# First attention of a macaron network on one core: the scores of the first 128 keys move into one product for four heads, and VectorE takes over the sum of maxima and queries

## The reference, cut to what matters

```
Q, K, V = heads(xn @ Wq), heads(xn @ Wk), heads(xn @ Wv)      # xn = layernorm(x)
scores  = einsum('bhqd,bhkd->bhqk', Q, K) * 8 ** -0.5
scores  = where(key > query, -1e6, scores)
attn    = einsum('bhqk,bhkd->bhqd', softmax(scores), V)
x       = x + attn @ Wo + bo
```

## Time and profile before

| | |
|---|---|
| median of 3 runs | 2064.63 us (2064.27 to 2064.72) |
| the profiled execution, and its span | 2066.3 us, 2064.3 us |
| busy share of the span | PE 96%, DVE 79%, ACT 58%, POOL 45% |
| attn0 | 331 to 711 us; a chunk inside the stage takes 45.8 us |

### The profile page before, as it was taken

The page is one execution under the profiler, slowest core; times in us unless marked ns, Lnnn a source line. Parts: engine busy times, 40 slices in busy tenths (PEclk is TensorE's granted clock), DMA queues, the critical chain, the costliest instruction groups (busy, mean ns, idle before and its releaser), DMA issues.

```text
span 2064.3 us, 44740 instructions
## 1 busy us (share of the span) xinstructions
PE 1985.8 (96%) x10752; PEld 1438.8 (70%) x10752; DVE 1632.7 (79%) x3337; ACT 1200.7 (58%) x1736; POOL 930.1 (45%) x904
## 2 busy tenths in 40 slices
PE   6999998999999999999999999998999999999998
PEld 4777776666666677777877888874333357787787
DVE  7777777777777577777588888886777788888887
ACT  6667664555555577676554445445767764454544
POOL 4665663333332366666544444442122334444444
PEclk9999999999999999999999999999999999999999
DMA  6333343333232243444311111114233301111112
GB/s 210 101 122 113 108 120 112 98 97 96 82 91 82 55 130 118 130 129 114 112 37 47 41 46 46 45 43 138 84 130 104 120 28 46 47 46 41 41 51 72
DMA packets 120701, 179.29 MB, mean 87 GB/s; under 512 B 33840, under 2 KB 38576, under 8 KB 120496
## 3 DMA queue, kind: packets, MB, share of 16 engines
q1 hardware_dynamic: 120624, 178.37, 29.3%
HBM read 147.10 MB, written 31.20 MB: 86 GB/s over the span
## 4 chain that ended last, share of the span: by engine, by line
PE 64%; DVE 11%; issue 11%; POOL 9%; ACT 3%; DVEq 1%; POOLq 1%; DMA 0%; SPq 0%; ACTq 0%
PE pair L397 14%; PE pair L399 13%; PE pair L398 13%; POOL h_lo L1364 6%; PE bank L651 5%; PE pair L740 3%; PE bank L629 3%; PE pair L762 3%; PE pair L823 2%; PE bank L397 2%; PE bank L399 1%; PE bank L398 1%; DVE rmax L1188 1%; DVE h_hi L1131 1%; POOL rstd L1284 1%
## 5 line engine op out<-in xcount | busy, mean ns | idle before, releaser
L1370 POOL TENSOR_TENSOR h_lo<-hid,h_hi 128x512 fp32r<-128x512 f32 x256 | 335.5, 1311 | 410.4 <-ACT h_hi L920 410.1
L397 PE MATMUL pair<-xnT_hi,w_hi 128*128 (+1 forms) x1040 | 420.0, 404 | 2.6 <-DVE prod L1110 1.3
L1364 POOL TENSOR_TENSOR h_lo<-hid,h_hi 128x512 fp32r<-128x512 f32 x256 | 332.3, 1300 | 194.6 <-ACT h_hi L886 193.4
L399 PE MATMUL pair<-xnT_hi,w_lo 128*128 (+1 forms) x1040 | 407.7, 392 | 0.0
L398 PE MATMUL pair<-xnT_lo,w_hi 128*128 (+1 forms) x1040 | 407.4, 392 | 0.0
L915 ACT ACTIVATE hid<-pair,bias 128x512 f32<-128x512 f32 x256 | 176.6, 690 | 315.5 <-PE pair L399 273.8
L397 PE MATMUL pair<-h_hi,w_hi 128*128 128x512 f32 x784 | 311.5, 397 | 14.5 <-DVE h_lo L1133 6.2
L399 PE MATMUL pair<-h_hi,w_lo 128*128 128x512 f32 x784 | 306.5, 391 | 0.0
L398 PE MATMUL pair<-h_lo,w_hi 128*128 128x512 f32 x784 | 305.9, 390 | 0.0
L1131 DVE TENSOR_SCALAR h_hi<-pair,nb 128x512 fp32r<-128x512 f32 x256 | 191.2, 747 | 69.8 <-PE pair L399 67.1
L938 ACT ACTIVATE probs<-pair 128x1024 f32<-128x1024 f32 x160 | 163.5, 1025 | 130.2 <-PE pair L762 127.0
(11 more groups left out here) (164 smaller groups left out, 3234.4 us busy)
## 6 DMA issues: line engine op xcount, KB each, us to landing
wb<-parts_dram SPq DMA_DIRECT2D x512, 128.0 KB, 2.9
wb<-parts_dram SPq DMA_DIRECT2D x128, 256.0 KB, 3.3
parts_dram<-attn_parts SPq DMA_DIRECT2D x96, 256.0 KB, 2.9
attn_q_st<-parts_dram SPq DMA_DIRECT2D x64, 256.0 KB, 2.7
k_one<-parts_dram SPq DMA_DIRECT2D x128, 64.0 KB, 2.5
attn_k_st<-parts_dram SPq DMA_DIRECT2D x32, 256.0 KB, 3.0
stage_w<-in_w_dram SPq DMA_DIRECT2D x32, 130.0 KB, 2.4
stage_w<-in_w_dram SPq DMA_DIRECT2D x5, 512.0 KB, 6.6
```

The source lines that it names most:

```text
L397: eng.matmul(o, w_hi_, v_hi, start=start, stop=False, **kw)
L399: return eng.matmul(o, w_lo_, v_hi, start=False, stop=stop, **kw)
L1364: eng.tensor_tensor(h_lo[:, p % NH0, :], hid[:, unit_of(p) % NHID, :] if p else hs[:, :], h_hi[:, p % NH0, :].bitcast(F32), ALU.subtract). ...
L1370: eng.tensor_tensor(h_lo[:, j % NH1, :], hid[:, j // 2 % NHID, :], h_hi[:, j % NH1, :].bitcast(F32), ALU.subtract).then_inc(lo1p_ready, 1)
```

## The change

- Fills 2 and 3 by query keep block 2 against 384 keys and lose block 0. Each fill of two heads is now two products, and fill 4 two products of 512 columns, each over two heads, in place of four of 256.
- Block 0 of all four heads is one product of 512 columns and one mask product of 512 (`first_block_by_query`). It goes into bank 1 of the pair whose bank 0 takes the maxima's rows, which was unused. DVE reduces it (`first_block_maximum`).
- `maxima_to_rows` loses its product with the identity; DVE adds the rows in PSUM to `q_st` in place (`rows_to_stack`), and ACT's copy goes.
- The maxima's step moves to the end of slots 3, 8, 13 and 18. It carries the rows of the quad as before, and the first block of the quad after it. Its pair is free again when DVE has reduced the first block.

```diff
-Q_FILLS = ((0, ((3, 0),)), (1, ((3, 0),)), (0, ((2, 0), (0, 384))), (1, ((2, 0), (0, 384))), (None, ((1, 0),)))
+Q_FILLS = ((0, 3), (1, 3), (0, 2), (1, 2), (None, 1))
-MAX_AT = (4, 9, 14, 19)
-USES = tuple(u for n in range(NS0) for u in (("q", n),) + ((("max", n),) if n in MAX_AT else ()) + (("k", n),))
+MAX_AT = (3, 8, 13, 18)
+USES = tuple(u for n in range(NS0) for u in (("q", n), ("k", n)) + ((("max", n),) if n in MAX_AT else ()))
...
+            for half in range(2):
+                if fill == NF - 1:
+                    both = pair[b][:, half, :].rearrange("p (h s) -> p h s", h=2)
+                    eng.matmul(both, q, mem0.k_one[:, quad, half:QUAD:2, 0:w], start=True, stop=True, skip_group_check=True)
+                else:
+                    eng.matmul(pair[b][:, half, 0:w], q, mem0.k_one[:, quad, 2 * Q_FILLS[fill][0] + half, 0:w],
+                               start=True, stop=True, skip_group_check=True)
...
+        def first_block_by_query(eng, ch, quad, b):
+
+            o = pair[b][:, 1, :].rearrange("p (h s) -> p h s", s=P)
+            eng.matmul(o, mem0.q_st[:, quad, 0:P], mem0.k_one[:, quad, :, 0:P], start=True, stop=True, skip_group_check=True)
+            eng.matmul(o, identb, neg.unsqueeze(1).broadcast_to([P, QUAD, P]), start=False, stop=True, skip_group_check=True).then_inc(s0_ready, 1)
+
         def maxima_to_rows(eng, ch, quad, b):
 
             eng.wait_ge(neg_max.sem, 2 * (NQ * ch.g + quad + 1))
-            eng.matmul(pair[b][:, 0, :], ident_r[:, :], mem0.q_st[:, quad, :], start=True, stop=False, skip_group_check=True)
...
+            if n in MAX_AT and in_chunk(ch, ("max", n)):
+                eng.wait_ge(*last_reader(ch, ("max", n)))
+                maxima_to_rows(eng, ch if max_quad(n) < NQ else ch.after(), max_quad(n) % NQ, ring(("max", n)))
+                if first_block_of(ch, n) is not None:
+                    first_block_by_query(eng, *first_block_of(ch, n), ring(("max", n)))
...
-            eng.activation(mem0.q_st[:, quad, :], pair[b][:, 0, :], ACT.Copy).then_inc(q_full, 1)
...
-                eng.tensor_reduce(q[:, 2, heads], src[:, :, 0:384], AX_X, ALU.max)
-                eng.tensor_reduce(q[:, 0, heads], src[:, :, 384:S], AX_X, ALU.max).then_inc(s_used, 1)
+                qt = Q_FILLS[fill][1]
+                eng.tensor_reduce(q[:, qt, heads], src[:, :, 0:(qt + 1) * P], AX_X, ALU.max).then_inc(s_used, 1)
...
+        def first_block_maximum(eng, ch, quad, b):
+
+            eng.wait_ge(s0_ready, NQ * ch.g + quad + 1)
+            eng.tensor_reduce(mem0.rmax[:, quad % 2, 0, :], pair[b][:, 1, :].rearrange("p (h s) -> p h s", s=P),
+                              AX_X, ALU.max).then_inc(s0_used, 1)
+
+        def rows_to_stack(eng, ch, quad, b):
+
+            eng.wait_ge(q_ps, NQ * ch.g + quad + 1)
+            eng.tensor_tensor(mem0.q_st[:, quad, :], pair[b][:, 0, :], mem0.q_st[:, quad, :].bitcast(F32), ALU.add).then_inc(q_full, 1)
```

More of the change, by code:

```diff
@@ L125, with first_block_quad @@
 PUT_AT = {"attn0": (11, 13, 18, 3), "attn1": (9, 10, 15, 2)}
-Q_FILLS = ((0, ((3, 0),)), (1, ((3, 0),)), (0, ((2, 0), (0, 384))), (1, ((2, 0), (0, 384))), (None, ((1, 0),)))
+Q_FILLS = ((0, 3), (1, 3), (0, 2), (1, 2), (None, 1))
 K_FILLS = ((0, ((0, 0),)), (1, ((0, 0),)), (0, ((1, P), (3, 0))), (1, ((1, P), (3, 0))), (None, ((2, 0),)))
 LOAD = 1024
-MAX_AT = (4, 9, 14, 19)
-USES = tuple(u for n in range(NS0) for u in (("q", n),) + ((("max", n),) if n in MAX_AT else ()) + (("k", n),))
-AHEAD_USES = tuple((what, n - NS0) for what, n in USES if n >= NS0 - AHEAD and what != "k" and (what, n) != ("max", MAX_AT[-2]))
+MAX_AT = (3, 8, 13, 18)
+USES = tuple(u for n in range(NS0) for u in (("q", n), ("k", n)) + ((("max", n),) if n in MAX_AT else ()))
+AHEAD_USES = tuple((what, n - NS0) for what, n in USES if n >= NS0 - AHEAD and what != "k")
 def max_quad(n):
-    return (n + 1) // NF
+    return (n + 2) // NF
+def first_block_quad(n):
+    return max_quad(n) + 1
 def ring(use):
@@ L503, in stacks_in, with first_block_of @@
             return 32 * (ch.ga + 1) + 48 * (ch.g + 1 if ch.causal else NB)
+        def first_block_of(ch, n):
+            quad = first_block_quad(n)
+            if quad < NQ:
+                return ch, quad
+            return None if ch.last else (ch.after(), quad - NQ)
         def filled(ch, use):
@@ L525, in last_reader @@
                 what, n = max((u for u in AHEAD_USES if ring(u) == k % NPAIR), key=AHEAD_USES.index)
-                return (s_used, n + AHEAD + 1) if what == "q" else (q_full, 1)
+                return (s_used, n + AHEAD + 1) if what == "q" else (s0_used, first_block_quad(n) + 1)
             b = max(b for b in range(len(USES)) if b % NPAIR == k % NPAIR)
@@ L735, in scores_by_query @@
                 eng.wait_ge(st_in[quad], stacks_in(ch))
[L736 to L741, removed]
+            qt = Q_FILLS[fill][1]
+            w = (qt + 1) * P
+            q = mem0.q_st[:, quad, qt * P:w]
+            for half in range(2):
[5 more added lines that the diff above has]
+                               start=True, stop=True, skip_group_check=True)
             for half in range(2):
@@ L745, in scores_by_query @@
                 else:
[L746 to L749, removed]
+                    o = pair[b][:, half, w - P:w]
+                ins = eng.matmul(o, identb, neg if fill < NF - 1 else neg.unsqueeze(1).broadcast_to([P, 2, P]),
                                  start=False, stop=True, skip_group_check=True)
@@ L785, in pe_attn0 @@
                     if behind:
-                        eng.wait_ge(s_used if behind[-1][0] == "q" else q_full, behind[-1][1] + AHEAD + 1 if behind[-1][0] == "q" else 1)
+                        what_was, m_was = behind[-1]
+                        eng.wait_ge(*((s_used, m_was + AHEAD + 1) if what_was == "q" else (s0_used, first_block_quad(m_was) + 1)))
                     if what == "q":
@@ L789, in pe_attn0 @@
                     else:
-                        maxima_to_rows(eng, ch, 0, ring((what, m)))
+                        if max_quad(m) >= 0:
+                            maxima_to_rows(eng, ch, max_quad(m), ring((what, m)))
+                        first_block_by_query(eng, ch, first_block_quad(m), ring((what, m)))
             f, owner = n + AHEAD, ch
@@ L1214, in dve_attn0 @@
                         eng.memset(mx[:, :, :].bitcast(F32), 0.0).then_inc(mx_zeroed, 1)
+                    if ("max", f - AHEAD) in AHEAD_USES:
+                        if max_quad(f - AHEAD) >= 0:
+                            rows_to_stack(eng, ch, max_quad(f - AHEAD), ring(("max", f - AHEAD)))
+                        first_block_maximum(eng, ch, first_block_quad(f - AHEAD), ring(("max", f - AHEAD)))
             f = n + AHEAD
@@ L1219, in dve_attn0 @@
                 maximum(eng, ch.after(), f - NS0, ring(("q", n)))
+            if n in MAX_AT and in_chunk(ch, ("max", n)):
+                rows_to_stack(eng, ch if max_quad(n) < NQ else ch.after(), max_quad(n) % NQ, ring(("max", n)))
+                if first_block_of(ch, n) is not None:
+                    first_block_maximum(eng, *first_block_of(ch, n), ring(("max", n)))
             if n == HALF_AT["attn0"]:
```

18 lines of the change are left out of this document (6 added, 12 removed).

## The result

The changed kernel has a median of 2059.81 us (20 runs, 2055.15 to 2066.05), the kernel before in the same comparison 2064.68 us (20 runs, 2059.36 to 2069.72). The ratio is 0.9977, with a 95% interval of 0.9968 to 0.9986: faster by 4.9 us, where 10.9 had been forecast. The profiled execution took 2062.5 us (span 2060.6).

A forecast was written before the change was run, and what follows sets the result against it. PE was taken to set the pace, DVE its only near neighbour. PE's 17.4 us less waits (8 x 0.65, and 2) left 10.2; with start 0.4 and end 0.3, 10.9 us: 2054.0 us, 8-in-10 range 2047.0 to 2061.5.

The forecast's parts named there:

- two products of 384, start to start: PE, fills 2 and 3: two products of 384 columns take 0.355 us instead of 0.60 for four, saving 0.245 a fill.
- PE's own time a quad: PE, net of fills, identity and first block: 0.545 us less a quad, between 0.15 and 0.82; 17.4 us over 32 quads.
- slot 13: take_half stands behind DVE's new pair, so the next maximum ends later and a by-key product waits: 0.25 us lost a chunk.
- wait for xn: Slot 18 to slot 2: DVE's chain to xn holds PE's transposes, the wait growing to about 0.7 us; 0.4 lost a chunk.
- new step's wait for the exponential: The moved maxima's step waits for the exponential of the by-key fill three uses back: 0.06 us a quad, 2 in all.
- first by-key product: Start, ahead of the first chunk: this product comes at 344.0 instead of 345.56, adding 0.4 us to the gain.
- the one of 1.5 us a chunk for PE's waits on DVE: Sign of failure: the forecast is wrong if PE's waits on DVE exceed 1.5 us a chunk.
- The one that I had opened with: By-key product of slot 16 waits for DVE's last reduction of block 0: 12 times for 0.4 us in six chunks.
- Rival 2: Only the columns count: short products hide their loads, about 7 us before DVE's share, 3 to 4 after; 2061, chance 0.17.
- Rival 1: Everything is kept: the next quad's slack absorbs the waits of slots 13 and 2; gain 17.4 + 0.7, 2046.5, chance 0.13.
- Rival 3: DVE becomes the bound behind the new pair in slots 13, 18 and 3: 12 us slower, 2076, chance 0.07.
- Rival 4: The change doesn't do what it says: the maxima's step's new place eats the gain; 2064, chance 0.06.

The follow-up runs named there:

- e5: The kernel before, without the products of query block 0 in fills 2 and 3: chunk 44.91 us against 45.79, median 2061.27 us in one run.
- e3: The changed kernel with the identity product and ACT's copy back, first block's move kept: chunk 45.43 us, median 2061.36 us, ratio 0.9974 to the kernel before.
- e4: The kernel before without the identity product, DVE adding the rows in the old place: chunk 44.84 us, median 2060.96 us, ratio 0.9976.
- e8: The changed kernel with both take_half steps ahead of the new pair, and the first quad's rows on identity product and ACT: chunk 44.26 us, ratio 0.9944 to before.

## Why the prediction was wrong in size

The direction and the range held. The gain was forecast at 10.9 us and is 4.9; per chunk 1.28 and 0.61. The steps, in the prediction's order:

| step | forecast | measured |
|---|---|---|
| two products of 384, start to start | 0.355 | 0.46 (0.35 in slot 4) |
| fills 2 and 3 of a quad, with masks | -0.71 | -0.18 and -0.23 |
| rows without the identity | -0.30 | -0.27 (0.72 to 0.45) |
| first block, product and mask | +0.465 | +0.45 |
| PE's own time a quad | -0.545 | -0.20 (10.01 less the wait of 0.12, to 9.69) |
| the step's old wait for DVE | not in the sum | -0.66 a chunk |
| DVE a chunk | 37.3 | 37.26 |
| slot 13 | by-key product, 0.25 | products with the values, 0.6 |
| wait for xn | 0.7 | 0.77 |
| new step's wait for the exponential | 0.06 a quad | none |
| first by-key product | 344.0 | 343.82 |

**The step that failed is the first: "two are 0.355 ... Saved: 0.245".** In fill 3 the four products before take 0.63, the two after take 0.46: 0.17 is saved, not 0.245. The halving between 256 and 512 columns used rows in which the first product follows a long f32 product. In fill 3 the first follows small value products. The single instructions of the changed kernel show it taking 0.28 and the second 0.18. The four of before had the same 0.28 in their 0.63, and I had taken off 0.03 for it where 0.10 was right: without it the four take 0.53 and the two 0.35, as they do in slot 4. In fill 2 less is saved, 0.12 (0.58 to 0.46): its first product took 0.23 behind a by-key product of 128 columns and takes 0.28 behind the first block's mask. The masks go from 0.15 to 0.09 a fill, and the after-effect that I had counted as saved stays, since the next two products of 512 take 0.55 in both kernels (607.00 to 607.55 in the earlier trace rows, 591.90 to 592.45 in the changed one). So the two fills give 0.41 where 0.71 was forecast, and that is what the first block costs again (0.45). The forecast 0.545 a quad is 0.20. My own test, "wrong if two products of 384 cost over 0.45", was met, and so was the one of 1.5 us a chunk for PE's waits on DVE: the rows come to 1.6.

**The second failure is in the waits.** The one that I had opened with, for L1194, cost nothing. By the starts of one chunk of each kernel, PE's own work falls by about 0.95 us where 2.18 was forecast. The waits were forecast to cost 0.89 (0.65, and 0.06 four times). They cost some 0.35: 1.4 came, 0.9 at the products with the values and 0.5 for xn, and 1.06 went, 0.66 at the old place of the maxima's step, 0.2 at the by-key product of slot 3 and 0.2 at the last of the q, k and v products. For slot 13 I followed `take_half` as something that delays the reductions behind it, and priced the by-key product that waits for these at 0.25; no wait shows there. That `take_half` itself frees a bank for the products with the values was not in the list at all. By the waits view it costs 0.56 in slot 14 and 0.17 in slot 4, 0.72 a chunk over the six. That the step's move would save a wait was not in the list either. So some 1.2 was missing in PE's work and some 0.55 was saved in waits, and the 0.67 a chunk that the forecast was off is about their difference. That it was no more is luck.

Over 8 chunks it is 5.4 of the 6.0 us by which the forecast was off. The rest, some 0.6, was to come from the start and the end. The first by-key product did come 1.74 us earlier (343.82 against 345.56 in the earlier trace rows), but the 3.4 us behind it run at a granted clock of 0.50, the lower level of 1.2 GHz, where before the 1.8 us from 345.5 on ran at full clock. The kernel before has its visit to the lower level ahead of the chunks (a clock of 0.57 from 336 to 340), and behind it PE waits 1.67 us for DVE anyway; the changed one has it in the first chunk, where PE is busy 3.38 of the 3.4 us:

```profile
343.80:347.20 3.40, 3.38 (x11) 2.50 (x12) 2.05 (x5) 1.71 (x2) 0.00 (x0) 0.50 0.00 0
```

**What stood.** The wait for xn was forecast at about 0.7 and is 0.77; that PE's saving between slots 18 and 2 would be lost to it is borne out by the interval of 8.27 and 8.32. The cost of the four-head product was bracketed between 0.235 and 0.33 and is 0.28. The two new DVE operations take 684 and 682 ns:

```profile
L1234 DVE TENSOR_TENSOR attn_q_st<-pair,attn_q_st 128x512 fp32r<-128x512 f32 x25 | 17.1, 684 | 0.3 <-PE pair L793 0.3
L1228 DVE TENSOR_REDUCE rmax<-pair 128x4 f32<-128x512 f32 x25 | 17.0, 682 | 0.3 <-PE pair L787 0.3
```

**The rivals.** Rival 2, that only the columns count, was near in its number: it gave 2061 at a chance of 0.17, and the result is 2059.8. Its price is not borne out. The two products of 128 that a fill loses are worth 0.17 us by e5's starts, between my 0.245 and the columns alone. The Trainium skill, page "TensorE: Matmul & The Clock Gate", section "Back-to-back issue gap", gives an isolated gap that grows with the columns, an estimate of 0.11 us for these two products, and says that for small ones it counts too little, since it leaves out the weight load. The 0.17 agrees with the second half of that. What the trace shows is where the rest lies: a product of 128 takes 0.06 itself, and the 384 behind it takes 0.23, where it takes 0.18 behind another 384. Rival 1, that everything is kept, is out by the waits and by the 0.20 a quad. Rival 3, that DVE becomes the bound, was half a truth: its place was right (the queue behind the pair in slots 13 and 18), its size was 1.2 us for each of three places where it came to 0.56, 0.5 and 0.17. Rival 4 is out: the step waits for no exponential, and its new place gave time back.

## What to carry to other kernels

- When a group of products is priced by interpolation, compare groups that stand behind the same kind of instruction. The first product of a group may carry 0.1 us that all the others hide, and in fill 3 it was the same before and after the change.
- A period is not a price. Leaving out products shortened e5's chunk by 0.88 us where their own starts say 1.4, because a wait behind them grew. And the first block's move shortened e3's chunk by 0.36 without taking work off PE. Compare starts of the same group, and then look at what comes behind it.
- A wait that a matmul's row covers is in no list of waits. It shows as a start that comes later than the same pair of instructions elsewhere.
- When work is added to an engine's queue, list everything behind it that frees a buffer, and not only the results that someone computes with. Here the cheap repair was to let the step that frees a bank go ahead of the new work: 0.84 us a chunk with no instruction changed, more than the change itself had brought.
- A step that looks late because it stands in the wrong slot may be on a loop between two engines. Of three ways of easing the wait for xn two cost 0.9 and 1.2 us a chunk, and one gained 0.07.

## What the runs showed of the hardware

- An f32 product of 384 columns takes 0.18 us to the next start behind a product of 384 or 512 columns, 0.23 behind one of 128, and 0.26 to 0.28 behind a bf16 mask or small value products. I take the extra for its weight load, with nothing long ahead to cover it; no run tests that. Two of them behind a short instruction take 0.46, about what two of 512 take elsewhere (0.47).
- Two products of 128 columns between those of 384 are worth 0.17 us: 0.06 each, and 0.05 on the 384 behind the first of them (e5).
- One product of 512 columns that reads 128 keys of each of four heads costs 0.28 us behind the transposed maxima. The plain identity product of 512 columns takes 0.28 in e3 and 0.33 in the kernel before, so reading over four heads costs nothing that can be seen.
- Whether the addition of the rows runs on DVE or as a product with the identity and a copy on ACT is worth 0.95 us a chunk where PE sets the pace (e4), and 0.07 the other way in the one slot where DVE is in the chain (e8).
